# Second attention's core: values of two heads per matmul in batches of four heads, a third place for exponentials, one VectorE pass per row tile

## The reference, cut to what matters

```python
q = _fq_sym(q * scale, axis=-1)        # round(x / s) * s, s = max|x| / 127 per head and token
k = _fq_sym(k, axis=-1)
v = _fq_sym(v, axis=2)                 # s per feature, over the keys
attn = softmax(einsum('bhqd,bhkd->bhqk', q, k))
attn = _fq_unsigned(attn, axis=-1)     # round(p / s) * s, s = max p / 255
out = einsum('bhqk,bhkd->bhqd', attn, v)
return out.reshape(B, N, C) @ Wp + bp
```

## Time and profile before

| | |
|---|---|
| median of 3 runs | 876.94 us (873.41 to 878.43) |
| the profiled execution | 876.02 us, of which the span of instructions is 874.3 us |
| the core of this attention | 291 to 482 us of the span |
| TensorE, matmul, over the span | 809.0 us busy (93%) |
| VectorE | 573.3 us (66%) |
| ScalarE | 387.0 us (44%) |
| GpSimd | 373.9 us (43%) |

### The profile page before, as it was taken

The page is one execution under the profiler, slowest core; times in us unless marked ns, Lnnn a source line. Parts: engine busy times, 40 slices in busy tenths (PEclk is TensorE's granted clock), DMA queues, the critical chain, the costliest instruction groups (busy, mean ns, idle before and its releaser), DMA issues.

```text
span 874.3 us, 15363 instructions
## 1 busy us (share of the span) xinstructions
PE 809.0 (93%) x5518; PEld 503.8 (58%) x5518; DVE 573.3 (66%) x1212; ACT 387.0 (44%) x668; POOL 373.9 (43%) x392
## 2 busy tenths in 40 slices
PE   7999999999999699999999979879999999999883
PEld 4647776544357256666666635445558967777531
DVE  4958876369664989999998597876621135124955
ACT  3244442311102689989999253646202343331211
POOL 3413403135153367777777261201170027971335
PEclk9999999999999799999999999989999999897998
DMA  9500001102510699999888300540853142991013
GB/s 288 113 0 2 1 1 47 45 0 46 112 36 1 115 172 165 160 154 168 164 161 151 76 1 1 124 132 2 194 165 118 49 139 61 258 247 34 16 13 36
DMA packets 217246, 82.33 MB, mean 94 GB/s; under 512 B 179506, under 2 KB 214990, under 8 KB 217182
## 3 DMA queue, kind: packets, MB, share of 16 engines
q1 hardware_dynamic: 214238, 76.23, 41.1%
q0 software_dynamic: 2944, 5.25, 2.6%
HBM read 33.21 MB, written 8.40 MB: 48 GB/s over the span
## 4 chain that ended last, share of the span: by engine, by line
PE 67%; DVE 10%; issue 7%; DMA 5%; POOL 5%; ACT 4%; SPq 2%; DVEq 0%; POOLq 0%; ACTq 0%
PE psum L1082 6%; PE psum L477 5%; PE psum L653 3%; DMA hT<-hT 3%; PE psum L1664 3%; PE psum L1107 3%; PE psum L633 3%; PE psum L516 3%; PE psum L1332 2%; PE psum L481 2%; PE psum L1109 2%; PE psum L1108 2%; DVE cx L2292 2%; PE psum L1942 2%; PE psum L457 2%
## 5 line engine op out<-in xcount | busy, mean ns | idle before, releaser
L1227 DVE TENSOR_SCALAR_CACHE_REDUCE psum<-psum,arena 128x1024 f32<-128x1024 f32 x128 | 164.6, 1289 | 14.5 <-PE psum L1082 14.0
L1188 POOL TENSOR_SCALAR hT<-arena 128x1024 f16<-128x1024 f32 x128 | 134.0, 1047 | 59.7 <-ACT arena L1162 41.9
L1162 ACT ACTIVATE arena<-psum,am 128x1024 f32<-128x1024 f32 x128 | 142.5, 1116 | 19.6 <-POOL hT L1188 10.6
L334 POOL TENSOR_TENSOR rstd<-ve,neg_half 128x1 f32<-128x1 f32 x64 | 39.5, 621 | 193.4 <-DVE ve L324 192.6
L1107 PE MATMUL psum<-hT,vaug 128*32 128x128 f16 x512 | 93.8, 222 | 2.8 <-DVE xT L1221 1.3
L1108 PE MATMUL psum<-m,arena 128*32 128x128 f16 x512 | 92.6, 220 | 0.0
L1109 PE MATMUL psum<-hT,vaug 128*32 128x128 f16 x512 | 92.5, 220 | 0.0
L1082 PE MATMUL psum<-arena 128*128 128x512 bf16 x256 | 78.8, 391 | 10.4 <-ACT arena L1162 9.1
L1107 PEld LDWEIGHTS psum<-hT,vaug 128*32 128x32 f16 x512 | 49.2, 96 | 50.3 <-issue 46.7
L711 POOL TENSOR_TENSOR arena<-arena,mask 128x1024 f32<-128x1024 f32 x16 | 30.0, 1900 | 56.3 <-PE psum L633 56.3
L1109 PEld LDWEIGHTS psum<-hT,vaug 128*32 128x32 f16 x512 | 49.8, 97 | 0.0
(11 more groups left out here) (405 smaller groups left out, 1755.0 us busy)
## 6 DMA issues: line engine op xcount, KB each, us to landing
hT<-in_L_ffn_expert_masks SPq DMA_DIRECT2D x32, 256.0 KB, 3.7
arena<-in_L_ffn_w_gate SPq DMA_DIRECT2D x2, 1408.0 KB
arena<-in_L_ffn_w_up SPq DMA_DIRECT2D x2, 1408.0 KB
arena<-in_L_ffn_w_down SPq DMA_DIRECT2D x2, 1408.0 KB
moe_in<-xT SPq DMA_DIRECT2D x2, 1024.0 KB, 7.1
hT<-moe_in SPq DMA_DIRECT2D x4, 512.0 KB, 5.9
moe_out<-arena SPq DMA_DIRECT2D x16, 128.0 KB, 1.7
hT<-hT SPq DMA_TRANSPOSE x112, 3.3
```

Source lines behind the costliest of these rows:

```text
L334: pool.tensor_tensor(rstd[:, t:t + 1], ve[:, t:t + 1], neg_half[:, t:t + 1], ALU.pow).then_inc(sig("ln_rstd"), 1)
L1162: act.activation(PE1[:, c % 2, :], psum[:, score_banks(c), :].rearrange("p a b -> p (a b)"), ACT.Exp, scale=-1.0, bias=am[:, bass.ds(n, 1) ...
L1188: pool.tensor_scalar(Y1[:, n % Y_SLOTS, :], PE1[:, n % 2, :], 255.0, 1024.0, ALU.mult, ALU.add)\
L1227: dve.tensor_scalar(s, s, size1[:, bass.ds(n, 1)], None, ALU.mult, ALU.min, accum_out=am[:, bass.ds(n, 1)])\
```

## The change

- V1 holds the values without zero columns. One matmul takes 32 value columns, those of two heads, against the turned weights of both heads (256 columns). Half of each result, one head's weights by the other's values, is not wanted.
- Values are computed for four heads at once (GROUP), in 24 matmuls that go alternately to two strips of PSUM rows. A batch is spread over four steps, six matmuls each; the last batch of a row tile over two, twelve each.
- A row tile's outputs fill a whole bank, two parts per head pair. VectorE multiplies all of it by the scales in one pass of 512 elements into `out_parts`, one step later than before. GpSimd then multiplies each part by the parity mask `par` (1 on the rows where the part is wanted, else 0) and adds them into xT (`add_parts`).
- One head of 16 (c % 16 = 7) is turned by TensorE; SP turns the 15 others. There are 12 places for turned heads; SP waits for a batch of values (`wait_values`). Landings are counted per Y1 place.
- The exponentials have a third place (`pe1`), and ScalarE waits for GpSimd's pass of head n - 3.
- The sum of value pairs goes from GpSimd to VectorE; clearing V1 goes away; the copies to V1 wait until all keys are turned.
- The late queries are quantised in four pieces after the passes of steps 3 to 6, and turned at step 20 instead of 10.
- In the steps below 11 TensorE issues two filler matmuls of 512 columns.
- ScalarE's wait before the scales, TensorE's before the turn and VectorE's before its inversion are adapted; the two waits for the end of the values (SP's and GpSimd's) count 64 increments instead of 128.

```diff
-        V1_pairs = a.tile([NB // 2, H, 2 * HD], FP16)
-        size1 = a.tile([P])
-        scale1, inv_wide = a.tile([DC, P]), a.tile([D])
-        V1 = Arena(vaug.rearrange("p t h d -> p (t h d)")).tile([NB, H, 2 * HD], FP16)
+        V1, V1_pairs = a.tile([NB, D], FP16), a.tile([NB // 2, D], FP16)
+        size1, inv_wide = a.tile([P]), a.tile([D])
...
-        PT_SLOTS, Y_SLOTS = 8, 4
-        PT1 = hT[:, 0:4, :].rearrange("p a n -> p (a n)").bitcast(FP16).rearrange("p (s k q) -> p s k q", s=PT_SLOTS, k=NB)
+        PT_SLOTS, Y_SLOTS = 12, 4
+        out_parts = qf.rearrange("p t d -> p (t d)")[:, 0:2 * DC * P].rearrange("p (c i q) -> p c i q", i=2, c=DC)
+        scale1 = qf[:, 2, :].rearrange("p (c q) -> p c q", c=DC)
+        PT1 = hT[:, 0:4, :].rearrange("p a n -> p (a n)").bitcast(FP16).rearrange("p (s k q) -> p s k q", k=NB, q=P)
+        PT1_late = xn.rearrange("p t d -> p (t d)").bitcast(FP16).rearrange("p (s k q) -> p s k q", k=NB, q=P)
...
-        TURN_EVERY, LAG_TURN, LAG_V = 8, 5, 8
-        TURN_AT, LAG_INVERT, LAG_REPEAT, LAG_SPREAD, LAG_OUT = 3, 3, 2, 6, 9
+        GROUP, TURN_AT, LAG_TURN, LAG_V = 4, 7, 5, 8
+        LAG_INVERT, LAG_REPEAT, LAG_SPREAD, LAG_OUT, LAG_ADD = 3, 2, 6, LAG_V + 2, LAG_V + 1
         LATE_PAIR = NB // 2 - 1
-        LATE_AT = {"round": 3, "repeat": 8, "turn": 10}
+        LATE_AT = {"round": 3, "repeat": 8, "turn": 20}
...
+            return sig(f"y1_slot{h % Y_SLOTS}_landed")
...
-            return c % TURN_EVERY == TURN_AT
+            return c % H == TURN_AT
 
         def wait_turned(eng, j, c):
 
-            each = 1 if by_tensor(c) else 16
-            eng.wait_ge(turned(c), j * (each * BODY // PT_SLOTS) + each * (c // PT_SLOTS + 1))
+            if by_tensor(c):
+                wait_step(eng, "y1_copied", row_tile(j, c))
+                return
+            slot = range(c % Y_SLOTS, NS, Y_SLOTS)
+            before, each = (sum(not by_tensor(h) for h in slot if h <= last) for last in (c, BODY - 1))
+            eng.wait_ge(turned(c), j * (16 * each) + 16 * before)
 
         def wait_turn_pe(eng, j, c):
 
-            eng.wait_ge(sig("y1_turned"), j * (BODY // TURN_EVERY) + c // TURN_EVERY + 1)
+            wait_step(eng, "y1_turned", row_tile(j, c))
+
+        def wait_values(eng, j, c):
+
+            eng.wait_ge(sig("v1_done"), j * (2 * BODY // GROUP) + 2 * (c // GROUP + 1))
+
+        def pt1(c, heads):
+
+            s = c % PT_SLOTS
+            return PT1[:, s:s + heads, :, :] if s < 8 else PT1_late[:, s - 8:s - 8 + heads, :, :]
+
+        def pe1(c):
+
+            return PE1[:, c % 3, :] if c % 3 < 2 else sg.rearrange("p a b -> p (a b)")
...
+            def values(c0, k0, k1):
+                for k in range(k0, k1, 2):
+                    for which in range(3):
+                        for c in range(c0, c0 + GROUP, 2):
+                            chunk, rows = c % H // 8, slice(16 * (c % 8), 16 * (c % 8) + 32)
+                            part = slice(c % H * HD, c % H * HD + 32)
+                            o = psum[rows, OUT_BANK, chunk * 2 * P:(chunk + 1) * 2 * P]
+                            if which == 1:
+                                pe.matmul(o, V1_pairs[:, k // 2, part], bc(m1024.unsqueeze(1), [P, 2, P]), start=False, stop=False)
+                                continue
+                            at = k + which // 2
+                            mm = pe.matmul(o, V1[:, at, part], pt1(c, 2)[:, :, at, :], start=(at == 0), stop=(at == NB - 1))
+                            if at == NB - 1:
+                                mm.then_inc(sig("v1_done"), 1)
...
+                    if isinstance(j, int) and c < LAG_V + GROUP - 1:
+                        keep_clock(pe, psum[:, OUT_BANK, :], 2)
...
-                    if c % H == TURN_AT:
-                        wait_step(pe, "scale1_ready", row_tile(j, c) + -1)
+                    wait_step(pe, "o1_read", row_tile(j, c) + -1)
...
-                if m is not None:
-                    if isinstance(j, int) and m == 0:
+                if m is not None and c % GROUP == GROUP - 1:
+                    if isinstance(j, int) and m == GROUP - 1:
                         pe.wait_ge(sig("v1_pairs_ready"), 1)
-                    wait_turned(pe, j, c)
-                    if c % H == 0:
-                        wait_step(pe, "o1_ready", row_tile(j, c) + -1)
-                    chunk, rows = c % H // 8, slice(32 * (c % 8 // 2), 32 * (c % 8 // 2) + 32)
-                    o = psum[rows, OUT_BANK, chunk * P:(chunk + 1) * P]
-                    first, last = c % 2 == 0, c % 2 == 1
-                    for k in range(0, NB, 2):
-                        pe.matmul(o, V1[:, k, c % H, :], PT1[:, c % PT_SLOTS, k, :], start=(first and k == 0), stop=False)
-                        pe.matmul(o, V1_pairs[:, k // 2, c % H, :], m1024, start=False, stop=False)
-                        mm = pe.matmul(o, V1[:, k + 1, c % H, :], PT1[:, c % PT_SLOTS, k + 1, :],
-                                       start=False, stop=(last and k == NB - 2))
-                    mm.then_inc(sig("v1_done"), 1)
+                    if c % H == GROUP - 1:
+                        wait_step(pe, "o1_read", row_tile(j, c) + -1)
+                    for i in range(GROUP):
+                        wait_turned(pe, j, c - i)
+                for i in range(GROUP):
+                    m, c = trails(j, c0, LAG_V + i)
+                    if m is not None and c % GROUP == GROUP - 1:
+                        parts = 2 if c % H == H - 1 else GROUP
+                        if i < parts:
+                            values(c - GROUP + 1, i * NB // parts, (i + 1) * NB // parts)
...
-                wait_step(act, "y1_ready", n + -2)
-                act.activation(PE1[:, c % 2, :], psum[:, score_banks(c), :].rearrange("p a b -> p (a b)"), ACT.Exp,
+                wait_step(act, "y1_ready", n + -3)
+                act.activation(pe1(c), psum[:, score_banks(c), :].rearrange("p a b -> p (a b)"), ACT.Exp,
...
-            pool.tensor_tensor(V1_pairs, V1[:, 0::2, :, :], V1[:, 1::2, :, :], ALU.add).then_inc(sig("v1_pairs_ready"), 1)
+            def add_parts(t):
+
+                pool.wait_ge(sig("o1_read"), t + 1)
+                for i in range(2):
+                    pool.tensor_scalar(out_parts[:, :, i, :], out_parts[:, :, i, :], par[:, i:i + 1], None, ALU.mult)\
+                        .then_inc(sig("o1_masked"), 1)
+                pool.wait_ge(sig("o1_masked"), 2 * (t + 1))
+                pool.tensor_tensor(xT[:, :, t * P:(t + 1) * P], out_parts[:, :, 0, :], out_parts[:, :, 1, :], ALU.add)\
+                    .then_inc(sig("o1_ready"), 1)
+
             for n in range(NS):
                 wait_step(pool, "p1_ready", n)
                 if n >= Y_SLOTS and by_tensor(n - Y_SLOTS):
                     wait_turn_pe(pool, 0, n - Y_SLOTS)
                 elif n >= Y_SLOTS:
                     wait_turned(pool, 0, n - Y_SLOTS)
-                pool.tensor_scalar(Y1[:, n % Y_SLOTS, :], PE1[:, n % 2, :], 255.0, 1024.0, ALU.mult, ALU.add)\
+                pool.tensor_scalar(Y1[:, n % Y_SLOTS, :], pe1(n), 255.0, 1024.0, ALU.mult, ALU.add)\
                     .then_inc(sig("y1_ready"), 1)
-                t, h = divmod(n - LAG_REPEAT, H)
-                if t >= 0 and h == H - 1:
-                    repeat_inverse(t)
+                for lag, work in ((LAG_REPEAT, repeat_inverse), (LAG_ADD, add_parts)):
+                    t, h = divmod(n - lag, H)
+                    if t >= 0 and h == H - 1:
+                        work(t)
             repeat_inverse(NB - 1)
+            add_parts(NB - 1)
...
-            dve.wait_ge(sig("v1_zeroed"), 1)
+            dve.wait_ge(sig("k1_turned"), 16 * 2 * NB)
             for i in range(2):
                 bank = ring_v.take(dve).bitcast(BF16)
-                ring_v.release(dve.tensor_copy(
-                    V1[:, 4 * i:4 * i + 4, :, :].rearrange("p k (r a) (b d) -> p (k r) (a b) d", a=2, b=2)[:, :, 0::3, :],
-                    bank.rearrange("p (k r a d) -> p (k r) a d", k=4, r=H // 2, a=2)))
+                n = ring_v.release(dve.tensor_copy(V1[:, 4 * i:4 * i + 4, :], bank.rearrange("p (k c) -> p k c", k=4)))
+            dve.wait_ge(ring_v.evacuated, n)
+            dve.tensor_tensor(V1_pairs, V1[:, 0::2, :], V1[:, 1::2, :], ALU.add).then_inc(sig("v1_pairs_ready"), 1)
...
-                    wait_step(dve, "v1_done", m)
+                    wait_values(dve, j, c)
                     wait_step(dve, "scale1_ready", t)
-                    dve.tensor_tensor(xT[:, :, bass.ds(t * P, P)], psum[:, OUT_BANK, 0:DC * P].rearrange("p (c q) -> p c q", c=DC),
-                                      scale1, ALU.mult).then_inc(sig("o1_ready"), 1)
+                    wait_step(dve, "o1_ready", t + -1)
+                    read = dve.tensor_tensor(out_parts, psum[:, OUT_BANK, :].rearrange("p (c i q) -> p c i q", c=DC, i=2),
```

(12 more changed lines are left out.)

35 lines of the change are left out of this document (22 added, 13 removed).

## The result

The changed kernel took 888.85 us (median of four runs, 880.47 to 891.31) against 876.26 for the kernel before in the same series: a ratio of 1.017, 95% interval 1.010 to 1.024. It is slower; the forecast was 870 us, with 878 as its upper end. The profiled execution took 886.99 us, its span is 884.9.

The account below looks back on a forecast made before the run. The prediction took TensorE to bound the core, VectorE 8% behind. Start -3.0, row tiles -2.7 and -3.2, last ten heads -0.5, end +2.6, together -6.8 from 876.02, gave a median of 870 us; 8-in-10 range 861 to 878 us.

Parts of the forecast that it names:

- the last sentence on the end: Attention core: GpSimd's two scalings and sum, 1.6 us per row tile, lie in its idle time, busy 15.2 of 20 us.
- The sum of the core: Attention core: three row tiles 23.0 to 22.1 us, -2.7; three 22.68 to 21.6, -3.2; last ten heads -0.5.
- The transposes: SP's queue in the core: 15 x 1.40 = 21.0 us per row tile, deciding in the first half at 22.1.
- Values: TensorE's value matmuls: neighbours on two strips overlap, 0.11 us per round; TensorE's step falls from 1.31 to 0.96 us.
- Rival (4): Value matmuls: fp16 strips don't run side by side, TensorE keeps 1.31 us; 875 us, chance 0.05.
- rival (3): Core: the queue holds nothing and ScalarE's insertions hide, row tiles of 20.4 us; 860 us, chance 0.11.
- ScalarE's insertions: Loop of three score places: turned head 1.01 and scales 0.73 exceed the 0.29 us slack, 0.72 + 0.44 lost.
- The start: Up to the first spread of the sums: 32.8 against 35.8 us, with another 0.8 -3.8; 0.8 held back, -3.0.
- The end: Last batch and projection: longer batch and half clock, masks and sum hidden beside w3's load; +2.6 us, ends 0.6 and 4.5.
- The sum: Whole kernel: start, row tiles, last ten heads and end together -6.8 us, from 876.02 to 869.2; median 870 us.
- rival (1): Core: the transposes take TensorE's place entirely, 180 of 186 us; core gain 2 to 4; 874.5 us, chance 0.18.
- Rival (2): Core: TensorE streams less, its clock falls to 1.2 GHz, 0.37 us lost per head; 886 us, chance 0.07.

Follow-up runs that it names:

- sums_on_dve: The changed kernel with masking and adding of the output parts done by VectorE instead of GpSimd: 872.94 us, ratio 0.997 to the kernel before.
- folded: The changed kernel with the sums on VectorE and the masks folded into its reading of the bank: 873.48 us, ratio 1.001 to the kernel before.
- folded_two_tail: The changed kernel with sums on VectorE, masks in its bank read, fillers after the last scores, two heads of 16 turned by TensorE: 876.66 us, ratio 1.005.
- tail_fill: The changed kernel with filler matmuls behind the last scores, ahead of the last batch's wait and ahead of the projection: 883.99 us, ratio 1.013.
- after_again: The changed kernel itself, unaltered, timed once more in the third series: 884.96 us, ratio 1.014 to the kernel before.
- core_fill: The changed kernel with one filler matmul of 512 columns before the scores of every core step: 889.78 us, ratio 1.019 to the kernel before.

## Why the prediction was wrong, point by point

- **The step that failed** is the last sentence on the end: "In the core the same three operations (1.6 us per row tile) lie in GpSimd's idle time: it is busy 15.2 of 20 us." It failed twice. The size: 0.4 for a scaling was an estimate from a sum's 0.74; measured were 0.922 us each and 0.724 for the sum, 2.57 per row tile. And the cover: GpSimd's 4.8 idle us in 20 are not one stretch that can take 2.6 us. They lie ahead of single passes: over the core it waited for ScalarE 70 times and 41.9 us, once for 9.8 at the start and else 0.5 us each. What is queued behind the added operations was not asked: GpSimd's next pass, and SP, whose transposes then follow each other at 1.38 us with no room to make up a gap. sums_on_dve puts it at 16 us on the clock of the whole kernel, of which 1.6 x 7 = 11 in the row tiles.
- **The sum of the core** had a second hole. Without the three operations (sums_on_dve) the seven row tiles take 156.7 us, 1.1 less than before, where the forecast took 6.4 off. In the first half a row tile then takes (391.7 - 320.9) / 3 = 23.6 us against the forecast's 22.1, in the second (458.4 - 391.7) / 3 = 22.2 against 21.6. The two query transposes would make up about 0.9 of the 1.5 us in the first half: the prediction held back 0.8 us in all for them, and they hold SP for 2.8.
- **The transposes** were costed as an issue interval, 1.40 us, with 21.0 per row tile. The interval is right (1.38). The prediction then let the queue decide only in the first half; in folded the transposes all but fill the row tile in the whole core, which stays at 22.16. On this the prediction set the Trainium skill's sentence that issue time is usually small relative to the DMA itself ("DMA: Bandwidth & Descriptors", Issuing engines are not separate DMA queues) against the row. The trace bears the row out: an issue takes 1.23 us with the DMA engines at rest, of 3.3 to landing.
- **Values** on TensorE: right. Pairs start together, rounds 0.11 us, a step 1.00 for the 0.96 forecast. Rival (4) is out, and rival (3) too, since no version came to its row tiles of 20.4 us.
- **VectorE** at 1.21 between stalls: right; its passes start at 313.96 and 315.16 us:

```profile
313.96 1.29 DVE L1284 TENSOR_SCALAR_CACHE_REDUCE psum<-psum,arena 128x1024 f32<-128x1024 f32 x1 [0.23 <-PE psum L1122]
...
315.16 1.29 DVE L1284 TENSOR_SCALAR_CACHE_REDUCE psum<-psum,arena 128x1024 f32<-128x1024 f32 x1
```

- **ScalarE's insertions** as a cost in the loop of three places: right in kind. folded_two_tail shows that a second one gives back at least what a transpose less gains.
- **The start**: forecast -3.8, with 0.8 held back; measured -5.7 at the first spread (326.9 to 321.2), of which 4.9 are lost again by the second, more than the 0.8 held back. The clock at 300 to 303 us is 1.00, as forecast.
- **Fetches**: the q8 row of the core counts 6, the number forecast.
- **The end**: forecast +2.6, bounds 0.6 and 4.5. Last spread to the next stage's first normalisation: 495.02 - 484.7 = 10.3 us before, 506.02 - 489.4 = 16.6 after, so +6.3. It has four parts. From the spread to the last landing +1.3 (1.1 to 2.4), which the sum didn't have. The last batch +1.9 (0.9 to 2.8), as the prediction's 0.6 and 1.3 add up to. Load and sum of w3 +0.2. From there to the normalisation +2.9 (2.6 to 5.5), for the 1 to 2 given to the projection: at half clock a tile takes 2.3 us instead of 1.27. The masks took 2.57 us with their sum where 1.5 were forecast, but that they are hidden beside load and sum was right as long as the clock was full (tail_fill). In after_again, where the last batch ran at the full clock, the whole stretch takes 505.56 - 491.2 = 14.4, so +4.1.
- **The sum**: -5.7 at the start, +10.4 in seven row tiles, +6.3 at the end, -0.4 behind it, gives the +10.6 of the spans. Forecast for the same parts were -3.0, -6.4 and +2.6.
- **The rivals**: rival (1) had the right resource, the transposes, and a gain all the same; its 874.5 us does not follow from its terms either (876.9 less 2 to 4 plus 2.6 is 875.5 to 877.5). Rival (2), the only slower one, gave 886 us, close to the measured time, by a mechanism that core_fill refutes. GpSimd's pause was on no list.

What stays open: whether the masks' pause ahead of the projection is what kept the clock at half there, whether SP's issues or the DMA engines would bound the transposes next, and why the spans behind this stage differ by several us between kernels that are alike there.

## What to carry to other kernels

Before moving work to an engine "with idle time", look at what it feeds: if that queue already issues back to back (here a transpose every 1.38 us), a pause of its feeder is not made up, however idle the feeder is on average: 2.6 us of added work cost 1.6 us per row tile here. Price an operation by a row of the same engine, type and shape, not by a cheaper relative. Look at the single intervals and not only at their mean: here the first of seven row tiles took nearly half of the loss, in part because two transposes had moved into it. And when one bound is lifted, read the shares of all queues and DMA engines in the same window before giving the difference to the next engine.

## What the runs showed of the hardware

- GpSimd's multiplication of 256 f32 elements per partition by a per-partition scalar, in place, takes 922 ns, longer than its 724 ns for adding two such tiles.
- VectorE's passes over 256 elements in SBUF vary with what GpSimd does beside them: the mask alone took 346 ns to 1102 ns in sums_on_dve (mean 635, above), 353 with GpSimd at rest; the plain sum in folded took 419 to 1080. The pass out of PSUM with the same mask and a second operand took 472 to 483 ns all 16 times. The mean of 635 ns says little about such an operation.
- SP issues back-to-back transposes of 256 KB from SBUF to SBUF every 1.38 us, in packets under 512 B. One issue with the DMA engines at rest takes 1.23 us.
- Value matmuls of 256 fp16 columns on two strips of 32 rows overlap fully: 0.11 us for two, and 0.21 us for two at a clock of 0.50.
